# Causal mask added by VectorE instead of a TensorE product, row maximum subtracted by GpSimd, two engine orders rearranged, in one attention layer of a decoder kernel

## The chip, the cores and the metric

The kernel runs on one core of one Trainium2 chip. The core has TensorE (PE: matmuls, and PEld for its weight loads), VectorE (DVE), ScalarE (ACT), GpSimd (POOL) and the queue engine SyncE (SP), each with an instruction queue of its own that is worked off strictly in order. They meet only at semaphores. The metric is device time in microseconds (us) of one launch; lower is better.

## The reference, cut to what matters

Two decoder layers with a layer norm after every residual sum. The fourth and the fifth of the six blocks are attentions of 16 heads of 16 elements, over 16 sequences of 128 tokens and 256 channels. The fourth has no mask; the fifth reads keys and values from a context and is causal:

```python
q = x @ Wq.T;  k = context @ Wk.T;  v = context @ Wv.T        # split into 16 heads
scores = jnp.einsum('bhqd,bhkd->bhqk', q, k) * SCALE
causal = jnp.tril(jnp.ones((t, kv_t), dtype=bool))
scores = jnp.where(causal[None, None, :, :], scores, -jnp.inf)
probs = jax.nn.softmax(scores, axis=-1)
y = jnp.einsum('bhqk,bhkd->bhqd', probs, v)
return y.transpose(0, 2, 1, 3).reshape(b, t, c) @ Wo.T + bo
```

Then `x = layernorm(x + y)`. All of it is fp32.

## The kernel before, in words

Each block is a round of 16 turns, one sequence each. The two attentions are round D (`n == 0`, no mask) and round E (`n == 1`, causal). They are written by one piece of code and run as one unbroken pipeline: `chained` walks through iterations, and in iteration i each engine runs its list of stages in the order of that list, a stage of lag L on turn i - L. So the position in an engine's list is its queue order within an iteration, and the lags say which of the five sequences in flight a stage belongs to. Buffers named with `[t.p]` are double; PSUM banks are not: bank 1 takes the projections of q and k, bank 2 v and the output projection, banks 3 to 6 the scores of four heads each (r = 0 to 3), bank 7 the transposed probabilities, bank 0 the weighted values.

One turn goes through these stages, with lags in brackets:

- `turn_x` (0) transposes x, `copy_xT` (0) copies it out; `d_proj_` (1) computes q and k, `d_qkc_` (1, ScalarE) copies them out in four instructions, `d_kx_` (1, GpSimd) expands k.
- `d_scores_` (2): in round E four mask products first, line 1232 (identity times the causal table, both bf16, 512 columns each, one for each bank), then 16 products with 32 rows, line 1237, which add to the banks.
- `d_max_(r)` (2, VectorE), for r = 0 to 3: the maximum over a row from the bank (line 1986), then the bank minus the maximum into `d_S` in SBUF (line 1989).
- `d_exp_(r)` (r = 0, 1, 2 at lag 2, r = 3 at lag 3; ScalarE, line 1557): exponential in place.
- `d_pT_(r)` (3, TensorE, line 1251): four transposes into bank 7. `d_pTc_(r)` (3, ScalarE, line 1564) copies bank 7 out. There is one bank 7, so `d_pT_(r + 1)` waits for `d_pTc_(r)`.
- `d_pv_` (3, line 1261) multiplies with v into bank 0; `d_oTc_` (4, ScalarE, line 1571) copies it out; `d_back_` (4) transposes it back; `d_div_` (4, VectorE, lines 1997 and 1999) divides by the row sums; `d_atp_`, `d_atc_`, `d_out_` (4) make the output projection; `d_y_` (4, VectorE) adds the residual (line 2007) and then runs the statistics of the layer norm (lines 1664, 1673); `ln_power` (4, GpSimd, lines 781 and 783) takes the root; `ln_final` (4, VectorE, line 1681) normalises.

TensorE's list per iteration, which the change leaves as it is, is: transposes r = 0 (lag 3), projection (1), back (4), transposes r = 1 (3), scores (2), atp (4), transposes r = 2 (3), v (1), transposes r = 3 (3), output projection (4), turn of x (0), pv (3). ScalarE's list ends with `d_exp_(2)`, and the next iteration begins with `d_oTc_` and `d_pTc_(0)`. GpSimd's list is copy of x, `d_xb_` (residual plus bias), `d_kx_`, `ln_power`.

SyncE issues loads of inputs and weights for later rounds during round E; they hang on semaphores that the change does not touch, apart from one small table (`rid`) whose semaphore is merged into another.

Of the kernel before, what the change touches and what calls it, by code (L numbers as in the profile page):

```python
# [268 lines left out]
def build(nc, a):  # L269
    out = a["out"]  # L270
    with ExitStack() as ctx:
# [16 lines left out]
        ident_bf = sb("ident_bf", [P, P], BF16)  # L288
        causal_bf = sb("causal_bf", [P, P], BF16)
# [199 lines left out]
        l_rid = sem("l_rid")  # L489
# [110 lines left out]
        d_max = step("d_max", 2 * NQ)  # L600
        d_exp = step("d_exp", NQ)
# [57 lines left out]
        def _(sp):  # L659
# [40 lines left out]
            sp.dma_start(rid[:], a["rid"]).then_inc(l_rid, 16)  # L700
# [66 lines left out]
        def _(pool):  # L767
# [104 lines left out]
            pool.wait_ge(l_rid, 16)  # L872
# [43 lines left out]
        def _(pe):  # L916
# [276 lines left out]
            for n, round in enumerate((D_, E_)):  # L1193
# [31 lines left out]
                def d_scores_(t, n=n):  # L1225
                    wait(pe, d_kxc.again(n), t, KC)
                    wait(pe, d_qkc.again(n), t, 4)
                    for r in range(NQ):
                        o = bank[3 + r]
                        wait(pe, d_max.again(n), t, 2 * (r + 1), back=1)  # L1230
                        if n == 1:
                            pe.matmul(o[:].rearrange("p (a b) -> p a b", a=QH), ident_bf[:],  # L1232
                                      causal_bf[:].unsqueeze(1).to_broadcast([P, QH, P]), start=True, stop=False)
                    for k in range(KC):
                        for r in range(NQ):
                            part = slice(32 * r, 32 * r + 32)
                            m = pe.matmul(bank[3 + r][:, k * D:(k + 1) * D], d_qT[t.p][part, k, :],  # L1237
                                          d_kx[t.p][part, k].rearrange("p a b -> p (a b)"), start=n == 0,
                                          stop=n == 0 or k == KC - 1)
# [99 lines left out]
            for i in range(B + 2):  # L1339
# [6 lines left out]
                if i == ROUTED_AFTER:  # L1346
                    pe.wait_ge(f_pre, 1)
                    pe.wait_ge(l_fc, 16)
# [44 lines left out]
        def _(act):  # L1393
# [146 lines left out]
            for n, round in enumerate((D_, E_)):  # L1540
# [39 lines left out]
                rounds.append([(d_oTc_, 4), (d_pTc_(0), 3), (d_exp_(3), 3), (d_qkc_, 1), (d_pTc_(1), 3), (d_atc_, 4),  # L1580
# [70 lines left out]
        def _(dve):  # L1651
# [37 lines left out]
            dve.tensor_copy(ident_bf[:], ident)  # L1689
            dve.tensor_copy(causal_bf[:], c("causal"))  # L1690
# [277 lines left out]
            for n, round in enumerate((D_, E_)):  # L1968
# [11 lines left out]
                def d_max_(r, n=n):  # L1980
                    dm = d_max.again(n)
                    def stage(t):
# [3 lines left out]
                        dve.tensor_reduce(mx, s_, AX.X, ALU.max).then_inc(dm.sem, 1)  # L1986
                        wait(dve, dm, t, 2 * r + 1)
                        wait(dve, d_pTp.again(n), t, NQ, back=2)
                        dve.tensor_tensor(d_S[t.p][:, QH * r:QH * (r + 1), :], s_,  # L1989
                                          mx.unsqueeze(2).to_broadcast([P, QH, P]), ALU.subtract).then_inc(dm.sem, 1)  # L1990
# [20 lines left out]
                rounds.append([(d_div_, 4), (d_max_(0), 2), (d_max_(1), 2), (d_max_(2), 2), (d_y_, 4), (d_max_(3), 2),  # L2011
# [36 lines left out]
            dve.wait_ge(l_fc, 16)  # L2048
# [215 lines left out]
```

## Time and profile before

| what | us |
|---|---|
| median of 3 runs | 1096.15 (1089.13 to 1096.21) |
| the profiled execution, its own time | 1097.09 |
| its span from first to last instruction | 1095.3 |
| PE busy | 930.2 (85%) |
| DVE busy | 593.5 (54%) |
| ACT busy | 444.4 (41%) |
| POOL busy | 432.5 (39%) |

Times in rows are microseconds from the start of the span, durations within a group of equal instructions are nanoseconds. Ends of matmuls are modelled, so consecutive PE rows overlap a little; the distance of two starts is the time that the first one really took from the queue.

### The profile page before, as it was taken

To read this page: it belongs to the slowest core of one execution; us is meant where nothing else is said; L and a number is where in the kernel's file an instruction comes from. 1 tells how busy PE (TensorE), PEld (TensorE's weight loads), DVE (VectorE), ACT (ScalarE), POOL (GpSimd) and SP (SyncE) were. 2 spreads that over 40 slices of the span, in tenths; PEclk is the share of its full clock that TensorE was granted. 3 is DMA by queue.
4 is the path that set the end of the run, shared out by engine and by line. 5 is a ranking of instruction groups with operands and counts; after the bars stand their busy time and mean duration, and the time that the engine had idled before them with its cause. 6 is when DMAs were issued, how large, how long until landed. Compare 5 with 4: busy or idle time off the path is not lost.

```text
span 1095.3 us, 20796 instructions
## 1 busy us (share of the span) xinstructions
PE 930.2 (85%) x5702; PEld 655.9 (60%) x5703; DVE 593.5 (54%) x1516; ACT 444.4 (41%) x1145; POOL 432.5 (39%) x678
## 2 busy tenths in 40 slices
PE   5888797784876899999999979989429999999980
PEld 2655686562754788888778757546205555555550
DVE  2898576647135888887778754731102222222224
ACT  2444332332201777776666644223203332233323
POOL 4799233200024233332223310067744554455553
PEclk8999997687585999999999986999759999999995
DMA  6500017900001000001322104023333445544546
GB/s 239 205 20 24 10 40 230 263 3 1 1 0 61 2 1 0 0 6 45 102 93 84 58 27 176 20 88 114 113 99 62 83 86 88 88 80 88 85 65 239
DMA packets 69845, 84.54 MB, mean 77 GB/s; under 512 B 16288, under 2 KB 61216, under 8 KB 69280
## 3 DMA queue, kind: packets, MB, share of 16 engines
q1 hardware_dynamic: 54624, 62.24, 18.8%
q0 software_dynamic: 14448, 19.01, 9.8%
q10 hardware_dynamic: 720, 2.63, 0.6%
q8 instruction: 26, 0.43, 0.2%
q14 instruction: 27, 0.22, 0.1%
HBM read 47.95 MB, written 36.24 MB: 77 GB/s over the span
## 4 chain that ended last, share of the span: by engine, by line
PE 65%; POOL 12%; DVE 8%; issue 7%; DMA 3%; ACT 2%; POOLq 0%; DVEq 0%; SPq 0%; ACTq 0%
PE bank L933 40%; PE bank L946 6%; POOL grid L886 6%; PE bank L1251 6%; PE bank L1237 3%; PE bank L1261 3%; PE bank L1232 1%; PE bank L1144 1%; POOL arena L803 1%; DMA inT<-in_xT 1%; POOL lr L783 1%; PE bank L925 1%; POOL arena L798 1%; POOL arena L797 1%; PE bank L1301 1%
## 5 line engine op out<-in xcount | busy, mean ns | idle before, releaser
L933 PE MATMUL bank<-arena 128*128 (+6 forms) x1248 | 416.5, 475 | 24.2 <-ACT arena L1444 10.5
L933 PEld LDWEIGHTS bank<-arena 128*128 128x128 f32 (+1 forms) x1248 | 229.4, 203 | 131.4 <-issue 87.8
L896 POOL DMA_INDIRECT ys<-arena x79 | 123.0, 1557 | 136.6 <-DVE arena L2155 127.5
L946 PEld LDWEIGHTS bank<-const,arena 128*128 128x128 f32 x636 | 77.3, 141 | 106.8 <-issue 99.1
L946 PE MATMUL bank<-const,arena 128*128 128x128 f32 x636 | 103.5, 277 | 37.6 <-DMA arena<-grid 32.3
L2147 DVE SCALAR_TENSOR_TENSOR arena<-arena,bank 128x256 f32<-128x256 f32 x79 | 38.0, 481 | 178.8 <-ACT arena L1627 178.8
L1986 DVE TENSOR_REDUCE arena<-bank 128x4 f32<-128x512 f32 x128 | 87.5, 683 | 37.4 <-PE bank L1237 37.2
L781 POOL TENSOR_TENSOR lr<-mv,const 128x1 f32<-128x1 f32 x80 | 15.2, 190 | 234.3 <-DVE mv L1673 234.3
L1627 ACT ACTIVATE arena<-bank 128x256 f32<-128x256 f32 x79 | 30.3, 383 | 174.6 <-PE bank L933 174.6
L933 PE MATMUL bank<-arena,inT 128*128 128x256 f32 (+1 forms) x256 | 85.3, 460 | 17.3 <-DMA inT<-in_xT 8.4
L1557 ACT ACTIVATE arena<-arena 128x512 f32<-128x512 f32 x128 | 80.9, 632 | 44.4 <-DVE arena L1989 40.7
L1989 DVE TENSOR_TENSOR arena<-bank,arena 128x512 f32<-128x512 f32 x128 | 88.6, 692 | 6.5
L933 PE MATMUL bank<-xT,arena 128*128 128x128 f32 x576 | 84.2, 295 | 5.2 <-ACT arena L1486 2.4
L1251 PE MATMUL bank<-const,arena 128*128 128x128 f32 x512 | 80.2, 280 | 2.8 <-ACT arena L1564 1.9
L933 PEld LDWEIGHTS bank<-xT,arena 128*128 128x128 f32 x576 | 75.9, 207 | 11.3 <-issue 5.3
L1564 ACT COPY arena<-bank 128x512 f32<-128x512 f32 x128 | 75.5, 590 | 8.0 <-PE bank L1251 4.4
L886 POOL DMA_INDIRECT grid<-arena x64 | 63.1, 986 | 27.0 <-issue 14.6
L1251 PEld LDWEIGHTS bank<-const,arena 128*128 128x128 f32 x512 | 56.5, 142 | 19.5 <-issue 18.0
L933 PEld LDWEIGHTS bank<-arena,inT 128*128 128x128 f32 x256 | 45.8, 198 | 34.7 <-issue 17.0
L853 POOL TENSOR_TENSOR arena<-arena,const 128x256 f32<-128x256 f32 x64 | 37.9, 612 | 35.3 <-ACT arena L1547 35.3
L2155 DVE COPY arena<-bank 128x256 f32<-128x256 f32 x79 | 33.6, 425 | 33.5 <-PE bank L933 33.5
L1416 ACT COPY xT<-bank 128x256 f32<-128x256 f32 x64 | 23.5, 367 | 65.9 <-DVE arena L1966 37.3
(259 smaller groups left out, 1371.7 us busy)
## 6 DMA issues: line engine op xcount, KB each, us to landing
arena<-in_f_w SPq DMA_DIRECT2D x18, 768.0 KB, 4.5
arena<-grid SPq DMA_DIRECT2D x79, 132.0 KB, 2.1
grid<-arena SPq DMA_DIRECT2D x1, 10112.0 KB, 33.2
inT<-in_ctxT SPq DMA_DIRECT2D x32, 128.0 KB, 2.0
arena<-ys SPq DMA_DIRECT2D x8, 512.0 KB, 6.3
inT<-in_xT SPq DMA_DIRECT2D x16, 128.0 KB, 2.1
X<-in_x SPq DMA_DIRECT2D x1, 2048.0 KB, 8.4
arena<-in_c_w SPq DMA_DIRECT2D x2, 1024.0 KB, 5.4
```

Source lines behind the costliest of these rows:

```text
L853: pool.tensor_tensor(d_kx[t.p][:, k], d_kT[t.p][:, k:k + 1, :].to_broadcast([P, 2, P]), c("pairs").unsqueeze(2).to_broadcast([P, 2, P]), A ...
L886: pool.indirect_dma_start(grid, bass.IndirectOffsetOnAxis(ap=f_to[:, b, k:k + 1], axis=0), f_sg[i][:, k, :], None).then_inc(l_sc[i], 16)
L896: pool.indirect_dma_start(ys, bass.IndirectOffsetOnAxis(ap=number, axis=0), s_y[t.ring(YR)], None, compute_op=ALU.add).then_inc(l_sy[t.rin ...
L933: m = pe.matmul(o, lhs[k], rhs[k], start=k == 0, stop=k == n - 1)
L946: m = pe.transpose(o[:, k * width:(k + 1) * width], src(k), ident[0:width, 0:width])
L1251: m = pe.transpose(bank[7][:, i * P:(i + 1) * P], d_S[t.p][:, QH * r + i, :], ident)
L1557: act.activation(v, v, ACT.Exp).then_inc(d_exp.sem, 1)
L1564: act.copy(d_pT[t.p][:, QH * r:QH * (r + 1), :], bank[7][:].rearrange("p (a b) -> p a b", a=QH)).then_inc(d_pTc.sem, 1)
L1986: dve.tensor_reduce(mx, s_, AX.X, ALU.max).then_inc(dm.sem, 1)
L1989: dve.tensor_tensor(d_S[t.p][:, QH * r:QH * (r + 1), :], s_, mx.unsqueeze(2).to_broadcast([P, QH, P]), ALU.subtract).then_inc(dm.sem, 1)
L2147: dve.scalar_tensor_tensor(out=f_a[0][:, t.p * EF:(t.p + 1) * EF], in0=f_h[t.p], scalar=s_x[t.ring(SR)][:, D:D + 1], in1=bank[2 + t.p][:, ...
L2155: dve.tensor_copy(s_y[t.ring(YR)], bank[6 + t.p][:, 0:D]).then_inc(q_yc.sem, 1)
```

## The change

The mask products of round E go, and with them the two bf16 tables and the two casts that filled them. In round E VectorE adds the causal table to the scores while it copies them from the bank to `d_S`, then takes the maximum from `d_S`; the subtraction becomes a new stage `d_sub_(r)` on GpSimd, in place in `d_S` (128 x 512), and the exponential waits for it. Round D keeps its two VectorE instructions. Both rounds take over new orders: VectorE does `d_y_` before `d_max_(2)` rather than after it; ScalarE does `d_qkc_` before `d_exp_(3)`. GpSimd's list becomes `d_sub_(3)` at lag 3, copy of x, `d_xb_`, `d_kx_`, `d_sub_(0)`, `d_sub_(1)`, `ln_power`, `d_sub_(2)`. The wait for `rid` is merged into that for `f_const`.

```diff
                 def d_scores_(t, n=n):
...
                     for r in range(NQ):
-                        o = bank[3 + r]
                         wait(pe, d_max.again(n), t, 2 * (r + 1), back=1)
-                        if n == 1:
-                            pe.matmul(o[:].rearrange("p (a b) -> p a b", a=QH), ident_bf[:],
-                                      causal_bf[:].unsqueeze(1).to_broadcast([P, QH, P]), start=True, stop=False)
...
+                def d_sub_(r, n=n):
+                    def stage(t):
+                        if n == 1:
+                            wait(pool, d_max.again(1), t, 2 * r + 2)
+                            v = d_S[t.p][:, QH * r:QH * (r + 1), :]
+                            pool.tensor_tensor(v, v, d_mx[t.p][:, QH * r:QH * (r + 1)].unsqueeze(2)
+                                               .to_broadcast([P, QH, P]), ALU.subtract).then_inc(d_sub.sem, 1)
+                    return stage
...
-                rounds.append([(copy_x(round, round - 1), 0), (d_xb_, 3), (d_kx_, 1), (ln_power(round), 4)])
+                rounds.append([(d_sub_(3), 3), (copy_x(round, round - 1), 0), (d_xb_, 3), (d_kx_, 1), (d_sub_(0), 2),
+                               (d_sub_(1), 2), (ln_power(round), 4), (d_sub_(2), 2)])
...
                 def d_exp_(r, n=n):
                     def stage(t):
-                        wait(act, d_max.again(n), t, 2 * r + 2)
+                        if n == 0:
+                            wait(act, d_max.again(0), t, 2 * r + 2)
+                        else:
+                            wait(act, d_sub, t, r + 1)
...
-                rounds.append([(d_oTc_, 4), (d_pTc_(0), 3), (d_exp_(3), 3), (d_qkc_, 1), (d_pTc_(1), 3), (d_atc_, 4),
+                rounds.append([(d_oTc_, 4), (d_pTc_(0), 3), (d_qkc_, 1), (d_exp_(3), 3), (d_pTc_(1), 3), (d_atc_, 4),
...
+                        v = d_S[t.p][:, QH * r:QH * (r + 1), :]
+                        if n == 0:
...
+                        else:
+                            wait(dve, d_pTp.again(n), t, NQ, back=2)
+                            dve.tensor_tensor(v, s_, c("causal").unsqueeze(1).to_broadcast([P, QH, P]), ALU.add)\
+                               .then_inc(dm.sem, 1)
+                            wait(dve, dm, t, 2 * r + 1)
+                            wait(dve, d_sub, t, NQ, back=2)
+                            dve.tensor_reduce(mx, v, AX.X, ALU.max).then_inc(dm.sem, 1)
...
-                rounds.append([(d_div_, 4), (d_max_(0), 2), (d_max_(1), 2), (d_max_(2), 2), (d_y_, 4), (d_max_(3), 2),
+                rounds.append([(d_div_, 4), (d_max_(0), 2), (d_max_(1), 2), (d_y_, 4), (d_max_(2), 2), (d_max_(3), 2),
                                (d_vc_, 1), (ln_final(round), 4)])
```

VectorE in round E, before, from the first maximum of an iteration on (banks 3 to 6 are r = 0 to 3, `y0` is the residual sum and waits for the output projection, `d_op`):

```order
L1986 TENSOR_REDUCE arena<-bank3 128x4 [waits d_sp]
L1989 TENSOR_TENSOR arena<-bank3,arena 128x512 [waits d_pTp,d_max]
L1986 TENSOR_REDUCE arena<-bank4 128x4 [waits d_sp]
L1989 TENSOR_TENSOR arena<-bank4,arena 128x512 [waits d_pTp,d_max]
L1986 TENSOR_REDUCE arena<-bank5 128x4 [waits d_sp]
L1989 TENSOR_TENSOR arena<-bank5,arena 128x512 [waits d_pTp,d_max]
L2007 TENSOR_TENSOR y0<-bank2,arena 128x256 [waits normed,d_xbc,d_op]
L1664 BN_STATS bn0<-y0 128x6 [waits d_y]
L1673 BN_AGGR mv0<-bn0 128x2 [waits rstd,stats]
L1986 TENSOR_REDUCE arena<-bank6 128x4 [waits d_sp]
L1989 TENSOR_TENSOR arena<-bank6,arena 128x512 [waits d_pTp,d_max]
```

and of the change, the same place (lines are numbered as in the changed kernel):

```order
L2000 TENSOR_TENSOR arena<-bank3,const 128x512 [waits d_pTp,d_sp]
L2004 TENSOR_REDUCE arena<-arena 128x4 [waits d_sub,d_max]
L2000 TENSOR_TENSOR arena<-bank4,const 128x512 [waits d_pTp,d_sp]
L2004 TENSOR_REDUCE arena<-arena 128x4 [waits d_sub,d_max]
L2021 TENSOR_TENSOR y0<-bank2,arena 128x256 [waits normed,d_xbc,d_op]
L1671 BN_STATS bn0<-y0 128x6 [waits d_y]
L1680 BN_AGGR mv0<-bn0 128x2 [waits rstd,stats]
L2000 TENSOR_TENSOR arena<-bank5,const 128x512 [waits d_pTp,d_sp]
L2004 TENSOR_REDUCE arena<-arena 128x4 [waits d_sub,d_max]
L2000 TENSOR_TENSOR arena<-bank6,const 128x512 [waits d_pTp,d_sp]
L2004 TENSOR_REDUCE arena<-arena 128x4 [waits d_sub,d_max]
```

The residual sum with its statistics has moved ahead of the pair on bank 5, and the add now comes ahead of the maximum.

ScalarE in round E, before, from `d_exp_(2)` at the end of one iteration into the next:

```order
L1557 ACTIVATE arena<-arena 128x512 [waits d_max]
L1571 COPY arena<-bank0 128x512 [waits d_bk,d_pv]
L1564 COPY arena<-bank7 128x512 [waits d_pv,d_pTp]
L1557 ACTIVATE arena<-arena 128x512 [waits d_max]
L1547 ACTIVATE arena<-bank1 128x128 [waits d_sp,d_kxc,d_qkp]
L1547 ACTIVATE arena<-bank1 128x128
L1550 ACTIVATE arena<-bank1 128x128 x2
L1564 COPY arena<-bank7 128x512 [waits d_pv,d_pTp]
```

and of the change:

```order
L1564 ACTIVATE arena<-arena 128x512 [waits d_sub]
L1578 COPY arena<-bank0 128x512 [waits d_bk,d_pv]
L1571 COPY arena<-bank7 128x512 [waits d_pv,d_pTp]
L1551 ACTIVATE arena<-bank1 128x128 [waits d_sp,d_kxc,d_qkp]
L1551 ACTIVATE arena<-bank1 128x128
L1554 ACTIVATE arena<-bank1 128x128 x2
L1564 ACTIVATE arena<-arena 128x512 [waits d_sub]
L1571 COPY arena<-bank7 128x512 [waits d_pv,d_pTp]
```

The exponentials (now line 1564) wait for GpSimd; the one of r = 2 still stands last in the iteration, ahead of the two copies that open the next; the one of r = 3 has moved behind the four copies of q and k.

GpSimd in round E, of the change, one iteration (before, it held only lines 773, 861, 853, 781 and 783, which are 771, 868, 851, 779 and 781 here). The first row is `d_sub_(2)` of one iteration and `d_sub_(3)` of the next:

```order
L860 TENSOR_TENSOR arena<-arena 128x512 [waits d_max] x2
L771 COPY xs0<-X 128x256 [waits turned,normed]
L868 TENSOR_TENSOR arena<-X,rows 128x256 [waits normed,d_y]
L851 TENSOR_TENSOR arena<-arena,const 128x256 [waits d_qkc,d_sp]
L851 TENSOR_TENSOR arena<-arena,const 128x256
L860 TENSOR_TENSOR arena<-arena 128x512 [waits d_max] x2
L779 TENSOR_TENSOR lr0<-mv0,const 128x1 [waits normed,stats]
L781 TENSOR_TENSOR lr0<-lr0,const 128x1 [waits rstd]
```

Four subtractions of 512 columns have come in, the one of r = 2 behind `ln_power`.

## Rows read from the trace of the kernel before

**Rows 1.** Stretches of rounds D and E: length, busy PE, PEld, DVE, ACT, POOL; clock
```profile
356.00:490.00 134.00, 131.24 (x1447) 109.25 (x1446) 115.35 (x225) 104.17 (x230) 43.17 (x89) 1.00 0.01 2
492.00:634.00 142.00, 141.39 (x1487) 112.37 (x1485) 113.25 (x225) 95.81 (x224) 43.39 (x88) 1.00 0.23 74
```

**Rows 2.** Mask and score products: count, ns min/median/max, first and last start
```profile
L1232 PE MATMUL bank<-causal_bf,ident_bf x64: 378/379/380, 491.9 to 633.8; 128*128 128x512 bf16 x64
L1237 PE MATMUL bank<-arena x512: 373/374/479, 354.6 to 634.8; 32*128 32x256 f32 x171
```

**Rows 3.** Timeline of PE in round E: start, us, engine, line, tiles, count
```profile
559.27 1.15 PE L1237 MATMUL bank<-arena 32*128 32x256 f32 x16
...
562.45 1.03 PE L933 MATMUL bank<-arena 128*128 128x256 f32 x4
...
567.36 0.60 PE L1251 MATMUL bank<-const,arena 128*128 128x128 f32 x4
567.80 1.03 PE L1232 MATMUL bank<-causal_bf,ident_bf 128*128 128x512 bf16 x4
568.75 1.15 PE L1237 MATMUL bank<-arena 32*128 32x256 f32 x16
```

**Rows 4.** Timeline of DVE in round E, the same turn; brackets: idle before, releaser
```profile
560.43 0.69 DVE L1986 TENSOR_REDUCE arena<-bank 128x4 f32<-128x512 f32 x1 [1.39 <-PE bank L1237]
...
563.19 0.68 DVE L1986 TENSOR_REDUCE arena<-bank 128x4 f32<-128x512 f32 x1
563.91 0.69 DVE L1989 TENSOR_TENSOR arena<-bank,arena 128x512 f32<-128x512 f32 x1
564.52 0.41 DVE L2007 TENSOR_TENSOR y<-bank,arena 128x256 f32<-128x256 f32 x1
...
565.65 0.69 DVE L1986 TENSOR_REDUCE arena<-bank 128x4 f32<-128x512 f32 x1
```

**Rows 5.** Timeline of ACT in round E, exponential of r = 2 and what follows
```profile
564.63 0.63 ACT L1557 ACTIVATE arena<-arena 128x512 f32<-128x512 f32 x1 [0.43 <-DVE arena L1989]
...
565.64 0.59 ACT L1564 COPY arena<-bank 128x512 f32<-128x512 f32 x1
...
567.64 0.43 ACT L1547 ACTIVATE arena<-bank 128x128 f32<-128x128 f32 x2
...
568.26 0.61 ACT L1564 COPY arena<-bank 128x512 f32<-128x512 f32 x1
```

**Rows 6.** Timeline of PE in round D, from one group of scores to the next
```profile
422.56 1.15 PE L1237 MATMUL bank<-arena 32*128 32x256 f32 x16
...
423.92 0.60 PE L1251 MATMUL bank<-const,arena 128*128 128x128 f32 x4
...
425.75 1.03 PE L933 MATMUL bank<-arena 128*128 128x256 f32 x4
...
430.65 0.60 PE L1251 MATMUL bank<-const,arena 128*128 128x128 f32 x4
431.19 1.15 PE L1237 MATMUL bank<-arena 32*128 32x256 f32 x16
```

**Rows 7.** Timeline of ACT in round D, the same turn
```profile
427.93 0.63 ACT L1557 ACTIVATE arena<-arena 128x512 f32<-128x512 f32 x1 [0.43 <-DVE arena L1989]
...
430.93 0.61 ACT L1547 ACTIVATE arena<-bank,cols 128x128 f32<-128x128 f32 x2
...
431.93 0.60 ACT L1564 COPY arena<-bank 128x512 f32<-128x512 f32 x1
```

**Rows 8.** GpSimd: elementwise on 512 and on 256 columns: ns min/median/max, first and last
```profile
L803 POOL TENSOR_TENSOR arena<-arena x16: 1255/1451/1715, 14.3 to 105.6; 128x512 f32<-128x512 f32 x16
L853 POOL TENSOR_TENSOR arena<-arena,const x64: 611/612/615, 351.2 to 625.7; 128x256 f32<-128x256 f32 x64
```

**Rows 9.** Timeline, round D: normalisation on DVE beside GpSimd's add
```profile
430.61 0.59 DVE L1681 TENSOR_SCALAR X<-y,mv,lr 128x256 f32 x1
430.31 0.74 POOL L861 TENSOR_TENSOR arena<-X,rows 128x256 f32<-128x256 f32 x1
```

More of the change, by code:

```diff
@@ L287, in build @@
         cols = sb("cols", [P, N_COLS])
-        ident_bf = sb("ident_bf", [P, P], BF16)
-        causal_bf = sb("causal_bf", [P, P], BF16)
         xs = [sb(f"xs{i}", [P, D]) for i in range(2)]
@@ L488, in build @@
         l_inT = [sem("l_inT0"), sem("l_inT1")]
-        l_rid = sem("l_rid")
         l_fill = sem("l_fill")
@@ L600, in build @@
         d_max = step("d_max", 2 * NQ)
+        d_sub = step("d_sub", NQ)
         d_exp = step("d_exp", NQ)
@@ L699, in _ @@
             load_x(turn(7))
-            sp.dma_start(rid[:], a["rid"]).then_inc(l_rid, 16)
+            sp.dma_start(rid[:], a["rid"]).then_inc(l_fc, 16)
             sp.dma_start(c_mask, a["mask"]).then_inc(l_cw, 16)
@@ L871, in _ @@
             pool.wait_ge(f_tail.sem, 3)
-            pool.wait_ge(l_rid, 16)
+            pool.wait_ge(l_fc, 32)
             pool.wait_ge(l_fill, 16 * 4)
@@ L1237, in d_scores_ @@
                             m = pe.matmul(bank[3 + r][:, k * D:(k + 1) * D], d_qT[t.p][part, k, :],
-                                          d_kx[t.p][part, k].rearrange("p a b -> p (a b)"), start=n == 0,
-                                          stop=n == 0 or k == KC - 1)
+                                          d_kx[t.p][part, k].rearrange("p a b -> p (a b)"), start=True,
+                                          stop=True)
                             if k == KC - 1:
@@ L1347, in _ @@
                     pe.wait_ge(f_pre, 1)
-                    pe.wait_ge(l_fc, 16)
+                    pe.wait_ge(l_fc, 32)
                     flat = lambda v: v.rearrange("p b e -> p (b e)")
@@ L1688, in _ @@
             dve.wait_ge(l_const, 16)
-            dve.tensor_copy(ident_bf[:], ident)
-            dve.tensor_copy(causal_bf[:], c("causal"))
             dve.memset(f_fill, 0.0).then_inc(f_filled, 1)
@@ L1985, in stage @@
                         mx = d_mx[t.p][:, QH * r:QH * (r + 1)]
[L1986 to L1990, printed above, removed]
+                        v = d_S[t.p][:, QH * r:QH * (r + 1), :]
+                        if n == 0:
+                            dve.tensor_reduce(mx, s_, AX.X, ALU.max).then_inc(dm.sem, 1)
+                            wait(dve, dm, t, 2 * r + 1)
+                            wait(dve, d_pTp.again(n), t, NQ, back=2)
+                            dve.tensor_tensor(v, s_, mx.unsqueeze(2).to_broadcast([P, QH, P]), ALU.subtract)\
+                               .then_inc(dm.sem, 1)
+                        else:
+                            wait(dve, d_pTp.again(n), t, NQ, back=2)
+                            dve.tensor_tensor(v, s_, c("causal").unsqueeze(1).to_broadcast([P, QH, P]), ALU.add)\
+                               .then_inc(dm.sem, 1)
+                            wait(dve, dm, t, 2 * r + 1)
+                            wait(dve, d_sub, t, NQ, back=2)
+                            dve.tensor_reduce(mx, v, AX.X, ALU.max).then_inc(dm.sem, 1)
                     return stage
@@ L2047, in _ @@
             grp = lambda v: v.rearrange("p b (g e) -> p (b g) e", e=EPG)
-            dve.wait_ge(l_fc, 16)
+            dve.wait_ge(l_fc, 32)
             route(dve.tensor_tensor(f_s, f_sc, row("ebias").unsqueeze(1).to_broadcast([P, B, E]), ALU.add))
```

## Prediction, written before the changed kernel was run

> **What bounds the kernel now.** I read the stretches first. In both rounds TensorE is never idle (131.2 of 134 us, 141.4 of 142), VectorE is busy 86% and 80%, ScalarE 78% and 67%, GpSimd about 3 us a turn, at clock 1.00 [rows 1]. The starts of the products give the periods: round D from 354.6 to 491.9, 16 iterations, 8.58 us each; round E from 491.9 to 633.8, 15 iterations, 9.46 us each [rows 2]. The timeline of one turn says the same: scores to scores 9.48 us in E, 8.63 in D [rows 3, 6], and the four mask products hold TensorE for 567.80 to 568.75, 0.95 us [rows 3], which is the difference. So TensorE sets the end now, and it is the engine that is relieved.
>
> A busy share says nothing of how far the next limit is, so I then followed the ring that closes through the other engines. Take s, the start of the score products, as zero.
>
> Round E before: VectorE starts on bank 3 at 1.16 and on bank 5 at 3.92; that pair ends at 564.60, 5.33 [rows 4]. The exponential of r = 2 starts at 564.63, 5.36. Behind it in ScalarE's queue stand the copy of bank 0 and then the copy of bank 7, which starts 1.01 behind the exponential (565.64) and is over 1.60 behind it, at 566.23 or 6.96 [rows 5]. TensorE's transposes of r = 1 need that copy; they start at 567.36, 8.09 [rows 3]. The ring has 1.13 us of slack, and it returns to the scores 0.44 us behind 567.36, plus the mask's 0.95. In D the same exponential starts at 5.37 and the transposes at 430.65, again 8.09 [rows 6, 7].
>
> **The change part by part.**
>
> *Mask products gone.* -0.95 us an iteration on TensorE. If nothing else bound, E would run at 9.48 - 0.95 = 8.53.
>
> *VectorE's pairs.* Bank minus maximum (0.69) becomes bank plus table, maximum from the bank (0.68) becomes maximum from SBUF. No row shows that maximum here; bounds are 0.61, the distance from 563.91 to 564.52 at which a 512-column operation lets the next one start, and 0.69. I take 0.68, nothing gained. A pair stays 1.41 long (563.19 to 564.60) [rows 4].
>
> *The residual sum ahead of bank 5, in both rounds.* It waits for the output projection of its iteration, whose modelled end is 562.45 + 1.03 = 563.48, 4.21 behind s in E, and 426.78, 4.22, in D [rows 3, 6]. With 0.05 us to cross, it starts at 4.26. VectorE is there at 3.92 [rows 4], so it now idles 0.34 us, and then spends 564.52 to 565.65 = 1.13 us on sum and statistics. The pair on bank 5 starts at 4.26 + 1.13 = 5.39 instead of 3.92. Everything queued behind it on ScalarE (the exponential of r = 2, both copies) is later by 1.47, and the next transposes on TensorE wait for those copies.
>
> *The subtraction on GpSimd, E alone.* No row shows it. Nearest are 256 columns with broadcast operands at 0.612, so 1.22 for two, and 512 plain columns of two operands at 1.255 at best, 1.451 in the median, 1.715 at worst [rows 8]. I take 1.25, the undisturbed one, and 0.1 for the extra crossing; the range keeps 1.2 and 1.72. The Trainium skill (GPSIMD Engine Reference, Performance versus the Vector engine) has a two-input fp32 operation on GpSimd take 1.96 times VectorE's time; an estimate by it is 1.36 us, which would add 0.11 us an iteration to the sum. No run here shows that ratio.
> GpSimd's load becomes 3.0 + 4 x 1.25 = 8.0 us an iteration: under every period below, so its latency counts and not its throughput. In queue order, the one of r = 2 finds `ln_power` done before it.
>
> *Round E, summed.* Bank 5's pair ends at 5.39 + 1.41 = 6.80; subtraction to 8.15; exponential at 8.20 instead of 5.36; bank 7 copied at 8.20 + 1.60 = 9.80; transposes at 9.85 instead of 8.09; scores 0.44 later at 10.29. Against 9.48 this is +0.81 us: the stall of 1.76 eats the 0.95 and more.
>
> *Round D, summed.* By the same ring without GpSimd the exponential starts at 6.84 instead of 5.37, transposes at 8.49, +0.40. A longer ring runs through the other reordering. Behind the copy of bank 7 now stand the four copies of q and k, 430.93 to 431.93 = 1.00 us [rows 7], and then the exponential of r = 3, which used to fit into ScalarE's idle time. From the exponential of r = 2: +1.01 copy of bank 7, +1.51 q and k, +2.51 exponential, +3.05 second copy of bank 7, +3.65 done, +3.70 transposes of r = 2, then 423.92 to 426.78 = 2.86 us to the end of the output projection [rows 6], 0.05 to the residual sum, and 1.13 + 1.41 + 0.04 back to the exponential: 9.19 us. D goes from 8.63 to 9.19, +0.56. In E this ring takes 10.17 (the copies of q and k take only 567.64 to 568.26 = 0.62 there [rows 5]), so the first one binds.
>
> *The rest.* Two casts of 128 columns at the start and a merged semaphore: at most the 0.69 us of one 512-column operation [rows 4]; I count nothing, since it ends up in the rounding. Loads by SyncE in E have no wait that the change moves. Removing `d_exp_(3)` from in front of the copies of q and k helps `d_kx_`, which has an iteration of slack. At the end of E the last sequence runs without cover: +1.35 for its subtraction, +0.3 idle before it, -0.95 for its mask: +0.7.
>
> Sum: D has residual sums from its third interval on, 14 x 0.56 = 7.8; E 15 x 0.81 = 12.2; end 0.7; together +20.7 on the profiled execution's own 1097.09, 1117.8. That execution lies 0.94 over the median of the runs, so 1116.9; I say **1116.5 us**, slower by 1.9%.
>
> **The rivals.**
>
> *TensorE stays the bound (faster).* If the ring's additions were covered, E would run at 8.53: 15 x 0.95 = 14, and 1082 us. TensorE's unbroken busy time in rows 1 speaks for it. Against it: the ring must not grow by more than 1.13 - 0.95 = 0.18 us in E, and the subtraction alone is 1.25. Chance 0.10.
>
> *The additions half hold (no change).* If the residual sum did not wait (the output projection done by 3.92) and statistics overlapped, only GpSimd's 1.35 would count: E at 9.48 - 0.95 + 1.35 - 0.18 = 9.70, D 8.9, and 1096 + 3 + 4 = 1103. I find no row in favour; modelled ends of matmuls, which could be off by 0.2 us, are the only opening. Chance 0.11.
>
> *VectorE and GpSimd block each other (slower still).* In D the normalisation ran beside GpSimd's add of 430.31 to 431.05 and ended at 431.20, 0.15 behind it; its 0.59 us look like a wait for the neighbour [rows 9]. Now the maxima read SBUF while subtractions run. If they exclude each other, the maximum of r = 1, due at 3.3, waits until the subtraction of r = 0 ends near 3.95; the residual sum starts at 4.75 instead of 4.26, E takes 10.8, and the time is 1117 + 15 x 0.5 = 1124. The same result comes if the subtraction takes its 1.72: 15 x 0.47 = 7. For it: the 0.59, and the spread in rows 8. Against: a maximum has a single SBUF operand. Chance 0.17.
> The Trainium skill (SBUF — State Buffer, section SBUF: two separate sides) says that the two engines share one pair of ports, held for a whole instruction by a GpSimd operation or by a VectorE one that uses two SBUF inputs or a two-port mode. By that rule the normalisation waits and the maximum does not; the normalisation has cover here, since the division behind it waits for ScalarE's copy of bank 0 until 9.98, so the rule would leave the forecast where it is. Rows 9 agree with it for the normalisation.
>
> *The clock falls* because TensorE now idles 1 to 2 us an iteration. Both rounds were granted 1.00 without a gap [rows 1], so these rows cannot price it; it would act in the same direction as the third rival and shares its chance.
>
> **How the numbers follow.** Forecast 0.62, the others 0.10, 0.11, 0.17. Its own spread: subtraction 1.2 and maximum 0.60 give 15 x -0.13 = -2; half of D's effect -4; matmul ends 0.2 earlier in both rounds -6. So 1105 to 1120. The range takes in the blocked case with some room above and most of the no-change case below, and leaves out the faster one: 1101 to 1126. A measurement of this kernel tells 1% from no change. Faster 0.10; same 0.12 (the half-held case and a thin edge of the forecast); slower 0.78.
>
> **What would show it.** Right: scores to scores 10.3 us in E and 9.2 in D; ScalarE idle before the exponential of r = 2, released by GpSimd in E; TensorE idle before the transposes of r = 1 (line 1251) by 1.5 to 1.8 us in E and before those of r = 1 or 2 in D, released by ScalarE's bank 7 copy; VectorE idle about 0.3 us before the residual sum, released by TensorE. Wrong: if TensorE has no idle time in E and its period is near 8.5, the ring is not there; if D is still at 8.6, the reordering costs nothing and all of the loss or gain is E's; if the subtraction takes 1.5 us or more, or a maximum stretches beside it, the third rival holds.

## The result, and the profile after

The changed kernel takes 1123.8 us in the median of 4 runs (1119.18 to 1127.36) against 1095.8 us: 1.0268 times the time of before, 95% interval 1.0212 to 1.0323. The forecast was 1116.5 us, slower by 1.9%, in a range of 1101 to 1126. The profiled execution took 1127.36 us, 30.3 more than that of before; it is the longest of the four.

The stretches of rounds D and E in the changed kernel (columns as in [rows 1]):

```profile
356.00:499.00 143.00, 136.13 (x1445) 109.18 (x1444) 114.75 (x224) 100.97 (x227) 43.51 (x90) 1.00 0.01 2
499.00:661.00 162.00, 140.26 (x1462) 112.37 (x1460) 128.26 (x235) 96.01 (x230) 106.33 (x150) 0.98 0.19 65
```

and its score products (as in [rows 2]; the line of the mask products has no counterpart):

```profile
L1241 PE MATMUL bank<-arena x512: 374/374/792, 354.0 to 658.9; 32*128 32x256 f32 x171
```

TensorE, unbroken before, is now idle 6.9 us in D and 21.7 us in E. To see where the time lies, I take the starts of the 32 groups of score products (one group for each turn, so the distance of two is an iteration) from each kernel's timeline of TensorE, and the first transpose of the stage behind the attentions (line 1301 before, 1305 after). D is from the first group to the 17th (16 intervals), E from the 17th to the 32nd (15), the end from the 32nd to that transpose.

| us | D | E | end | steady iteration in D / E |
|---|---|---|---|---|
| before | 138.3 | 141.2 | 20.2 | 8.6 to 8.8 / 9.48 |
| changed | 147.4 | 156.1 | 26.5 | 9.3 to 9.5 / 10.4 |
| forecast for the change | +7.8 | +12.2 | +0.7 | 9.19 / 10.29 |
| measured | +9.1 | +14.9 | +6.3 | |

Together +30.2; D started 0.6 earlier than before, and the later stages add the same again.

One turn of round E follows, from the timelines of the changed kernel; rows between are left out where three dots stand. TensorE (before: [rows 3]):

```profile
563.18 1.15 PE L1241 MATMUL bank<-arena 32*128 32x256 f32 x16
...
566.36 1.03 PE L941 MATMUL bank<-arena 128*128 128x256 f32 x4
...
568.37 1.08 PE L1265 MATMUL bank<-arena 128*32 128x128 f32 x32 [0.76 <-ACT arena L1571]
...
572.46 0.66 PE L954 MATMUL bank<-const,arena 128*128 128x128 f32 x4 [0.64 <-ACT arena L1578]
573.04 0.63 PE L1255 MATMUL bank<-const,arena 128*128 128x128 f32 x4
573.63 1.15 PE L1241 MATMUL bank<-arena 32*128 32x256 f32 x16
```

VectorE (before: [rows 4]):

```profile
564.44 0.69 DVE L2000 TENSOR_TENSOR arena<-bank,const 128x512 f32<-128x512 f32 x1 [0.94 <-PE bank L1241]
...
566.60 0.69 DVE L2004 TENSOR_REDUCE arena<-arena 128x4 f32<-128x512 f32 x1
567.52 0.42 DVE L2021 TENSOR_TENSOR y<-bank,arena 128x256 f32<-128x256 f32 x1 [0.23 <-PE bank L941]
...
568.74 0.69 DVE L2000 TENSOR_TENSOR arena<-bank,const 128x512 f32<-128x512 f32 x1
569.46 0.69 DVE L2004 TENSOR_REDUCE arena<-arena 128x4 f32<-128x512 f32 x1
...
571.71 1.02 DVE L1688 TENSOR_SCALAR X<-y,mv,lr 128x256 f32 x1
```

GpSimd, the subtractions of r = 0, r = 2 and r = 3:

```profile
566.05 1.04 POOL L860 TENSOR_TENSOR arena<-arena 128x512 f32<-128x512 f32 x1 [1.77 <-DVE arena L2004]
...
570.23 1.04 POOL L860 TENSOR_TENSOR arena<-arena 128x512 f32<-128x512 f32 x1 [0.51 <-DVE arena L2004]
571.55 1.04 POOL L860 TENSOR_TENSOR arena<-arena 128x512 f32<-128x512 f32 x1 [0.28 <-DVE arena L2004]
```

ScalarE (before: [rows 5]):

```profile
571.30 0.63 ACT L1564 ACTIVATE arena<-arena 128x512 f32<-128x512 f32 x1 [1.97 <-POOL arena L860]
571.84 0.57 ACT L1578 COPY arena<-bank 128x512 f32<-128x512 f32 x1
572.30 0.59 ACT L1571 COPY arena<-bank 128x512 f32<-128x512 f32 x1
```

The ring (the chain of waits from TensorE's scores through the other engines' queues and back to TensorE) can be walked in these rows. A bracket gives the time from the scores at 563.18, and then the forecast. The residual sum waits for the output projection and starts at 567.52 (+4.34; 4.26). The pair on bank 5 starts 1.22 later and ends at 570.15 (+6.97; 6.80). GpSimd subtracts from 570.23 to 571.27 (+8.09; 8.15), the exponential of r = 2 starts at 571.30 (+8.12; 8.20; before 5.36). Bank 0's copy stands behind it, and TensorE, idle 0.64 us, takes up the transposes back when that is over, then those of r = 1 at 573.04 (+9.86; 9.85), then the scores at 573.63 (+10.45; 10.29). TensorE's wait stands one step ahead of where I had put it: before line 954, whose data is bank 0's copy, not before line 1255. Its size is also another. I had forecast 1.5 to 1.8 us in one place; there are two waits, this one of 0.64 us and one of 0.76 us before the product with v (line 1265), which waits for bank 7's last copy. The second belongs to another ring, which experiments 4 and 5 uncover.

Round D, changed kernel, TensorE's timeline and then ScalarE's (before: [rows 6, 7]):

```profile
425.51 0.65 PE L954 MATMUL bank<-const,arena 128*128 128x128 f32 x4 [0.31 <-ACT arena L1578]
426.09 0.63 PE L1255 MATMUL bank<-const,arena 128*128 128x128 f32 x4
426.73 1.15 PE L1241 MATMUL bank<-arena 32*128 32x256 f32 x16
```

```profile
424.35 0.63 ACT L1564 ACTIVATE arena<-arena 128x512 f32<-128x512 f32 x1 [2.13 <-DVE arena L1996]
```

Score products start at 417.26 and again at 426.73, 9.47 us later; the exponential of r = 2 waits 2.13 us for VectorE and starts 7.09 behind the scores, where it was 5.37 [rows 6, 7].

### The profile page after: what moved, and what is told of

It is laid out like the page before. It is cut to its first block, busy times and chain, and to the rows that moved or that the text cites. A ratio compares the mean times of both kernels' runs of the same rounds, so it can differ in the third digit from the quotient of the medians.

```text
span 1125.5 us, 20843 instructions
## 1 busy us (share of the span) xinstructions
PE 932.1 (83%) x5638; PEld 654.4 (58%) x5639; DVE 603.2 (54%) x1514; ACT 441.4 (39%) x1145; POOL 498.7 (44%) x742
## 4 chain that ended last, share of the span: by engine, by line
PE 51%; POOL 14%; DVE 12%; issue 11%; ACT 4%; DMA 1%; POOLq 1%; DVEq 0%; ACTq 0%; SPq 0%
PE bank L941 32%; PE bank L954 6%; POOL grid L894 6%; PE bank L1255 4%; PE bank L1241 3%; POOL arena L860 2%; POOL lr L781 2%; DVE bn L1671 2%; ACT arena L1578 1%; PE bank L1152 1%; DVE arena L1996 1%; DVE arena L1993 1%; DVE y L2021 1%; POOL arena L801 1%; PE bank L1305 1%
## 5 line engine op out<-in xcount | busy, mean ns | idle before, releaser
L954 PE MATMUL bank<-const,arena 128*128 128x128 f32 x636 | 106.8, 282 | 53.7 <-DMA arena<-grid 33.0
L1634 ACT ACTIVATE arena<-bank 128x256 f32<-128x256 f32 x79 | 30.3, 383 | 174.6 <-PE bank L941 166.0
L860 POOL TENSOR_TENSOR arena<-arena 128x512 f32<-128x512 f32 x64 | 66.7, 1043 | 47.1 <-DVE arena L2004 47.1
L1255 PE MATMUL bank<-const,arena 128*128 128x128 f32 x512 | 83.5, 287 | 3.3 <-ACT arena L1571 2.3
L941 PEld LDWEIGHTS bank<-xT,arena 128*128 128x128 f32 x576 | 76.7, 208 | 11.3 <-issue 5.3
L1571 ACT COPY arena<-bank 128x512 f32<-128x512 f32 x128 | 75.8, 592 | 11.3 <-PE bank L1255 9.0
L1993 DVE TENSOR_REDUCE arena<-bank 128x4 f32<-128x512 f32 x64 | 43.7, 682 | 17.9 <-PE bank L1241 17.5
L2000 DVE TENSOR_TENSOR arena<-bank,const 128x512 f32<-128x512 f32 x64 | 43.9, 686 | 16.4 <-PE bank L1241 16.4
L1688 DVE TENSOR_SCALAR X<-y,mv,lr 128x256 f32 (+1 forms) x80 | 42.9, 537 | 16.0 <-POOL lr L781 14.8
```

The source lines that it names most:

```text
L860: pool.tensor_tensor(v, v, d_mx[t.p][:, QH * r:QH * (r + 1)].unsqueeze(2) .to_broadcast([P, QH, P]), ALU.subtract).then_inc(d_sub.sem, 1)
L941: m = pe.matmul(o, lhs[k], rhs[k], start=k == 0, stop=k == n - 1)
L954: m = pe.transpose(o[:, k * width:(k + 1) * width], src(k), ident[0:width, 0:width])
L1255: m = pe.transpose(bank[7][:, i * P:(i + 1) * P], d_S[t.p][:, QH * r + i, :], ident)
L1571: act.copy(d_pT[t.p][:, QH * r:QH * (r + 1), :], bank[7][:].rearrange("p (a b) -> p a b", a=QH)).then_inc(d_pTc.sem, 1)
L1688: dve.tensor_scalar(o, y[t.p][:], mv[t.p][:, 0:1], lr[t.p][:, 1:2], ALU.subtract, ALU.mult)\
```

## Experiments

**1. VectorE's order alone, on the kernel before.**

```diff
-                rounds.append([(d_div_, 4), (d_max_(0), 2), (d_max_(1), 2), (d_max_(2), 2), (d_y_, 4), (d_max_(3), 2),
+                rounds.append([(d_div_, 4), (d_max_(0), 2), (d_max_(1), 2), (d_y_, 4), (d_max_(2), 2), (d_max_(3), 2),
```

> The kernel before, with one edit: VectorE does the residual sum and its statistics ahead of the pair on bank 5 (r = 2) in both rounds. Theory (the ring through ScalarE's queue): the exponential of r = 2 starts 7.1 us behind the scores instead of 5.4, the transposes of r = 1 about 1.74 behind it, scores again 0.6 later in D and 1.55 later in E, where the mask products stand between: D at 9.4 to 9.5 us an iteration, E at 10.2 to 10.4, 1118 to 1124 us in all. So this order alone would cost as much as the whole change. Rival (the order is harmless and the loss is GpSimd's): 1094 to 1099 us, periods of 8.6 and 9.5.

Measured: 1115.9 us, 1.0205 (1.0156 to 1.0254). D 147.8, E 151.5, iterations of 9.3 to 9.5 and of 10.0 to 10.1. The last interval of E, 11.2, is not among them. Its timelines of ScalarE and TensorE in E show the same ring without GpSimd:

```profile
574.57 0.63 ACT L1557 ACTIVATE arena<-arena 128x512 f32<-128x512 f32 x1 [1.91 <-DVE arena L1989]
575.11 0.57 ACT L1571 COPY arena<-bank 128x512 f32<-128x512 f32 x1
```

```profile
575.73 0.66 PE L946 MATMUL bank<-const,arena 128*128 128x128 f32 x4 [0.18 <-ACT arena L1571]
```

So one stage moved in a list costs 2%, and the rival, that the order is harmless, is out. In D it costs the whole of what the change costs there (147.8 against 147.4). The total came out 2 us under the expected range, since E's iteration was 10.05 where I had put 10.2 to 10.4.

**2. ScalarE's order alone, on the kernel before.**

```diff
-                rounds.append([(d_oTc_, 4), (d_pTc_(0), 3), (d_exp_(3), 3), (d_qkc_, 1), (d_pTc_(1), 3), (d_atc_, 4),
+                rounds.append([(d_oTc_, 4), (d_pTc_(0), 3), (d_qkc_, 1), (d_exp_(3), 3), (d_pTc_(1), 3), (d_atc_, 4),
```

> The kernel before, with one edit: ScalarE copies q and k (1.0 us in D, 0.62 in E) ahead of the exponential of r = 3, in both rounds. Theory: both stand ahead of bank 7's second copy in either order, so nothing changes: 1093 to 1098 us, D 8.6, E 9.5. Rival (the second step of the prediction for D, that this reordering lengthens a ring): D at 9.0 to 9.2 us and 1102 to 1106 us.

Measured: 1098.2 us, 1.0035 (1.0015 to 1.0054); D 141.8 with iterations of 8.96, E unchanged at 9.48. Neither theory was right as written: the first had no effect at all, the rival had 1102 to 1106 us. The reordering costs D 0.2 to 0.3 us an iteration, by a ring that neither had. ScalarE's timeline in D, then TensorE's one turn earlier:

```profile
428.36 0.62 ACT L1547 ACTIVATE arena<-bank,cols 128x128 f32<-128x128 f32 x2 [1.36 <-PE bank L933]
428.88 0.63 ACT L1550 ACTIVATE arena<-bank,arena 128x128 f32<-128x128 f32 x2
429.38 0.65 ACT L1557 ACTIVATE arena<-arena 128x512 f32<-128x512 f32 x1
429.89 0.60 ACT L1564 COPY arena<-bank 128x512 f32<-128x512 f32 x1
```

```profile
421.67 0.63 PE L1251 MATMUL bank<-const,arena 128*128 128x128 f32 x4 [0.15 <-ACT arena L1564]
```

ScalarE waits 1.36 us for the projection, then does the copies of q and k (1.0), the exponential of r = 3 and bank 7's copy, for which TensorE waits. In the kernel before, ScalarE did the exponential of r = 3 first:

```profile
430.40 0.63 ACT L1557 ACTIVATE arena<-arena 128x512 f32<-128x512 f32 x1 [0.88 <-DVE arena L1989]
```

It waited there for VectorE and began while the projection was just ending (modelled end 430.38, and in this experiment the copies start 0.19 behind that end), so about a third of it was hidden. The ring was nearly closed already: every second iteration of D took 8.78 before. In E the copies take 0.62 and the slack covers it.

**3. The changed kernel with VectorE's order of before.**

```diff
-                rounds.append([(d_div_, 4), (d_max_(0), 2), (d_max_(1), 2), (d_y_, 4), (d_max_(2), 2), (d_max_(3), 2),
+                rounds.append([(d_div_, 4), (d_max_(0), 2), (d_max_(1), 2), (d_max_(2), 2), (d_y_, 4), (d_max_(3), 2),
```

> The changed kernel with VectorE's order of before (residual sum behind the pair on bank 5). Theory: D returns to 8.6 us an iteration (13 us back). E does not: on GpSimd the layer norm's root stands ahead of the subtraction of r = 2 and now waits for statistics that come at 6.45 us behind the scores, so the subtraction runs from 7.3 to 8.4, and E takes 10.6 to 10.9 instead of 10.4. Together 1112 to 1118 us. Rival (VectorE's order is the whole loss): E at 8.9 and 1088 to 1096 us.

Measured: 1122.0 us, 1.0247 (1.0208 to 1.0286), 4 us over the expected range. E 161.8, iterations of 10.6 to 10.9 as expected; D 141.0 at 8.97, not 8.6, which is experiment 2's effect. The rival, that VectorE's order is the whole loss, is out: taking that order back wins 6 us in D and loses as much in E. GpSimd's timeline shows the queue (the last row holds the subtractions of r = 2 and r = 3), and VectorE's the normalisation:

```profile
575.87 0.19 POOL L779 TENSOR_TENSOR lr<-mv,const 128x1 f32<-128x1 f32 x1 [1.40 <-DVE mv L1680]
576.14 0.55 POOL L781 TENSOR_TENSOR lr<-lr,const 128x1 f32<-128x1 f32 x1
576.66 2.10 POOL L860 TENSOR_TENSOR arena<-arena 128x512 f32<-128x512 f32 x2
```

```profile
577.45 0.41 DVE L1688 TENSOR_SCALAR X<-y,mv,lr 128x256 f32 x1
```

Two small operations of a layer norm wait 1.40 us for statistics, and the subtraction of r = 2, ready at 574.67 where its maximum ended, starts at 576.66. With GpSimd's order as the change has it, the residual sum has to stand early on VectorE: the two orders belong together.

**4. As 3, and GpSimd subtracts r = 2 ahead of the layer norm.**

```diff
-                               (d_sub_(1), 2), (ln_power(round), 4), (d_sub_(2), 2)])
+                               (d_sub_(1), 2), (d_sub_(2), 2), (ln_power(round), 4)])
```

> As a_dve, and on GpSimd the subtraction of r = 2 ahead of the layer norm's root. Theory: the exponential of r = 2 starts at 6.5 us behind the scores, E takes 8.8 to 9.0 us an iteration, D 8.6, and the time is 1086 to 1093 us, faster than before. Rival (GpSimd's load and its collisions with VectorE bind E whatever the order): E stays over 9.5 us and the time over 1096.

Measured: 1095.0 us, 1.0001 (0.9978 to 1.0025), 2 us over the expected range. The loss is gone by two positions in two lists; the one on GpSimd's list alone is worth 27 us against experiment 3. D is at 8.96 again, and E comes to 9.46 where I expected 8.9. The next ring, in the timelines of ScalarE and TensorE:

```profile
566.09 0.63 ACT L1564 ACTIVATE arena<-arena 128x512 f32<-128x512 f32 x1 [1.37 <-POOL arena L860]
566.63 0.57 ACT L1571 COPY arena<-bank 128x512 f32<-128x512 f32 x1
```

```profile
567.34 1.08 PE L1265 MATMUL bank<-arena 128*32 128x128 f32 x32 [0.76 <-ACT arena L1571]
```

The exponential of r = 0 stands in front of bank 7's last copy; GpSimd's subtraction holds it 1.37 us, with it the copy behind it, and so the product with v on TensorE for 0.76 us. It is the same kind of ring, one place on, and its two waits stood in the changed kernel already, inside the longer iteration.

**5. The changed kernel, the exponential of r = 2 behind the two copies.** This is the one test with the subtraction in place in which VectorE's and GpSimd's orders stay as the change has them.

```diff
-                rounds.append([(d_oTc_, 4), (d_pTc_(0), 3), (d_qkc_, 1), (d_exp_(3), 3), (d_pTc_(1), 3), (d_atc_, 4),
+                rounds.append([(d_oTc_, 4), (d_pTc_(0), 3), (d_exp_(2), 3), (d_qkc_, 1), (d_exp_(3), 3), (d_pTc_(1), 3), (d_atc_, 4),
                                (d_pTc_(2), 3), (d_exp_(0), 2), (d_pTc_(3), 3), (d_exp_(1), 2),
-                               (copy_xT(round, before, reader, bank[1]), 0), (d_exp_(2), 2)])
+                               (copy_xT(round, before, reader, bank[1]), 0)])
```

> The changed kernel with one edit: on ScalarE the exponential of r = 2 runs at lag 3, behind the two copies (bank 0, bank 7) that TensorE's next products wait for. Theory (that exponential, late by VectorE's order and GpSimd's subtraction, holds the copies up): TensorE's waits before the transposes back (line 954) go. E then falls to the next ring, about 9.45 us an iteration (exponential of r = 0 in front of bank 7's last copy, TensorE waits 0.76 us before line 1265), D to 8.9 to 9.0 us. 1098 to 1104 us. Rival (the subtraction's time or its collisions bind as such, wherever the exponential stands): E stays at 10.2 to 10.5 and the time over 1115.

Measured: 1097.7 us, 1.0013 (0.9973 to 1.0054); D 141.1 at 8.96, E 139.8 at 9.45, and TensorE's only wait in E is the 0.76 us of experiment 4. A single stage of one engine, put behind two others, takes back the whole loss: the late exponential did its harm by standing ahead of two copies, not by being late.

**6. Without the subtraction.**

```diff
-                        if n == 1:
+                        if n == 2:
                             wait(pool, d_max.again(1), t, 2 * r + 2)
...
-                            wait(act, d_sub, t, r + 1)
+                            wait(act, d_max.again(n), t, 2 * r + 2)
...
+                        act.activation(v, v, ACT.Exp, scale=1.0 if n == 0 else 0.01).then_inc(d_exp.sem, 1)
...
-                            wait(dve, d_sub, t, NQ, back=2)
```

> The changed kernel without GpSimd's subtraction; the exponential waits for the maximum instead. It leaves out the subtraction of the maximum in round E and scales the exponential's argument by 0.01 there so that nothing overflows; all other instructions stand. Theory: the subtraction costs its own latency, 1.04 + 0.1 us, once an iteration on the ring: E 9.3 to 9.4 us, D unchanged at 9.4 to 9.5; 1103 to 1109 us. Also the normalisation on VectorE (1.02 us now) falls back to 0.4 to 0.6. Rival (VectorE's order alone sets E): E stays over 10 us, over 1115 in all.

Measured: 1105.4 us, 1.0106 (1.006 to 1.0153); E 138.7 at 9.25 to 9.33, D 147.4. So with these orders the subtraction on GpSimd costs 10.4 - 9.3 = 1.1 us an iteration, its 1.04 and one crossing (the time from one engine's end to the next one's start). The rest of E's loss, against the 8.62 that TensorE comes to in experiment 8, is order. The normalisation is back at 0.41, as expected.

**7. and 8. A ScalarE order for the new latency, and the normalisation moved.** The first has experiment 4's orders on VectorE and GpSimd, and this list in place of ScalarE's (the three lines that it replaces are left out):

```diff
+                rounds.append([(d_oTc_, 4), (d_pTc_(0), 3), (d_exp_(2), 3), (d_qkc_, 1), (d_pTc_(1), 3), (d_exp_(3), 3),
+                               (d_atc_, 4), (d_pTc_(2), 3), (d_pTc_(3), 3), (d_exp_(0), 2),
+                               (copy_xT(round, before, reader, bank[1]), 0), (d_exp_(1), 2)])
```

> a_dvepool with a ScalarE order for the subtraction's latency: bank 0's copy, bank 7's copy, exponential r = 2 (lag 3), q and k, bank 7's second copy, exponential r = 3, atp's copy, two copies of bank 7, exponentials r = 0 and r = 1. Theory: no exponential stands ahead of a copy for which TensorE waits before it is ready; D at 8.6 us, E limited by VectorE at 8.7 to 8.9 us (its instructions sum to 8.5 with the normalisation stretched to 1.0 beside GpSimd). 1082 to 1089 us, faster than before. Rival (there is another ring near 9.4 us): 1092 to 1097.

Measured: 1081.1 us, 0.9893 (0.985 to 0.9936), 1 us under the expected range. D 135.5 at 8.62; E 129.9, alternating 8.63 and 8.83. In E VectorE is now almost without a pause (3 us in the 110 from 510 us on), and one of its instructions runs beside a subtraction on GpSimd (timelines of the two):

```profile
563.43 1.02 DVE L1688 TENSOR_SCALAR X<-y,mv,lr 128x256 f32 x1
```

```profile
563.26 1.04 POOL L860 TENSOR_TENSOR arena<-arena 128x512 f32<-128x512 f32 x1 [0.51 <-DVE arena L2004]
```

The second moves that instruction one iteration on, to where VectorE waits for scores:

```diff
-                rounds.append([(d_div_, 4), (d_max_(0), 2), (d_max_(1), 2), (d_max_(2), 2), (d_y_, 4), (d_max_(3), 2),
-                               (d_vc_, 1), (ln_final(round), 4)])
+                rounds.append([(d_div_, 4), (ln_final(round), 5), (d_max_(0), 2), (d_max_(1), 2), (d_max_(2), 2), (d_y_, 4), (d_max_(3), 2),
+                               (d_vc_, 1)])
```

> best1 with the normalisation (line 1688) one iteration later, behind the division, where VectorE waits for scores anyway. Theory: if VectorE's stretched normalisation limits E in best1, E comes to 8.5 to 8.7 us, TensorE's own pace, 1080 to 1086 us. Rival: it does not limit, same as best1 within 2 us.

Measured: 1076.8 us, 0.9857 (0.9814 to 0.99), 3 us under the expected range; both rounds at 8.62 in every steady iteration, 135.5 and 128.5. In E the normalisation takes 0.41 and 0.57 in turn (VectorE's timeline, a short one):

```profile
562.52 0.41 DVE L1688 TENSOR_SCALAR X<-y,mv,lr 128x256 f32 x1
```

TensorE's timeline in the same iteration, the four transposes of r = 1 with the score products straight behind them:

```profile
561.68 0.60 PE L1255 MATMUL bank<-const,arena 128*128 128x128 f32 x4
562.21 1.15 PE L1241 MATMUL bank<-arena 32*128 32x256 f32 x16
```

**9. The same again, and a control.**

> best2 once more for a narrower interval: 1074 to 1080 us, 0.98 to 0.99 of the kernel before; D and E at 8.6 us an iteration.

Measured: 1077.4 us, 0.9831 (0.9798 to 0.9865).

The control has ScalarE's order and the place of the normalisation of experiment 8 on the kernel before, with the mask on TensorE and the subtraction on VectorE.

> The kernel before, mask products on TensorE and subtraction on VectorE, with the ScalarE order and the place of the normalisation of best2. Theory (TensorE limits E with the mask in it): E at 9.5 us, D at 8.6, 1091 to 1096 us; the gain of best2 then comes from the mask's removal and the orders only let it through. Rival (the orders alone bring it): 1078 to 1086 us.

Measured: 1090.8 us, 0.9952 (0.9926 to 0.9978). E stays at 9.48, D is at 8.62. So of the 18 us that experiment 8's kernel gains in this comparison, 5 are the orders and 13 come with the mask's removal: 15 x (9.48 - 8.62) = 12.9.

**10. The changed kernel again, for the end.**

> The changed kernel once more, unchanged. Question: where the last sequences of round E run without cover, TensorE took 26.5 us from its last scores to the first transposes of the next stage instead of 20.2, at a granted clock of 0.5 to 0.8. Theory A (the drop belongs to this kernel: its last full iterations idle 2.5 us, and the records fall to 0.50 right behind): again 24 to 27 us at a clock below 0.8, median 1119 to 1126 us. Theory B (which execution drops is chance): 19 to 21 us at a clock near 1.0, and a time near 1120 us.

Measured: 1122.9 us, 1.0251 (1.0214 to 1.0288). D 147.4 as in the first profile, E 155.3, 0.7 less and all of it in the last interval (10.24 against 11.01); the end took 22.3 us, between the two theories, so neither is right as written. Stretches of four microseconds of the first profile, then of this one (the third number from the right is the granted clock):

```profile
652.00:656.00 4.00, 1.54 (x26) 1.11 (x16) 3.71 (x6) 1.73 (x5) 3.12 (x5) 0.87 0.00 0
656.00:660.00 4.00, 4.00 (x26) 2.87 (x25) 1.17 (x3) 1.05 (x2) 0.37 (x1) 0.50 0.00 0
```

```profile
660.00:664.00 4.00, 1.67 (x36) 1.26 (x36) 3.73 (x8) 1.51 (x3) 2.60 (x5) 1.00 0.00 0
664.00:668.00 4.00, 2.62 (x14) 1.64 (x14) 0.68 (x2) 2.94 (x7) 1.46 (x2) 0.84 0.00 0
```

In the first the clock falls from full to half behind one wait of 2.46 us, at 655.5, in the second behind the second such wait, at about 666.5. The end is dearer than before in both, by 2.1 and 6.3 us, where I had said 0.7. The 4.2 us between the two executions go with the moment at which the clock falls. The kernel before loses clock there as well (0.66 to 0.81 from 642 us on), so its 20.2 holds some of it, and there the longest wait of TensorE up to the fall was 1.05 us.

## Why the prediction was right

**The direction and the place: right.** TensorE stopped being the bound, and the ring through ScalarE's in-order queue took over. Its stations were forecast within 0.17 us in E, in part by luck: errors of both signs cancel, as the next paragraphs show. The time alone would not have told. 1123.8 us lies above the forecast's own spread of 1105 to 1120, and on the 1124 of the third rival, whose mechanism the rows refute for the maxima.

**"The residual sum ahead of bank 5", +1.47 us on everything behind it: right, and 1.64.** The pair on bank 5 starts 5.56 behind the scores in E, where it was 3.92: the sum starts 0.08 later than forecast, and it takes 1.22 with its statistics where I had 1.13. Experiment 1 has this order alone: 1.0205, some 20 us. All of D's loss is its; in E, experiments 1 and 6 give 0.6 us an iteration to the order alone and 1.1 to the subtraction. Experiment 5 shows that both act through the queue.

**"The subtraction on GpSimd", 1.25 us: 1.04.** All 64 lie between 1.039 and 1.141, cheaper than both neighbours in [rows 8]; that is 1.5 times the 0.69 of VectorE's add, where the ratio of 1.96 that the prediction cites gives its 1.36. From the pair's end to the exponential it was 1.15 us instead of 1.40, an error of 0.25 in favour of the change.

**A missing term, the restart of TensorE.** Behind its wait the four transposes back take 0.58 us from start to start (572.46 to 573.04), where they take 0.44 in a full queue (566.92 to 567.36 before). With them the way from the exponential to the transposes of r = 1 is 1.74 instead of 1.65. The timelines of TensorE's weight loads show where it goes. Before, in the full queue, and then in the changed kernel, behind the wait:

```profile
566.81 0.47 PEld L946 LDWEIGHTS bank<-const,arena 128*128 128x128 f32 x4
```

```profile
572.46 0.42 PEld L954 LDWEIGHTS bank<-const,arena 128*128 128x128 f32 x4 [0.82 <-ACT arena L1578]
```

The loads ran 0.11 us ahead of the products (566.81 to 566.92); behind the wait both start at 572.46, since the loads wait for the same copy. That this lost lead is the whole 0.14 us is argued. The next four take 0.59, where I used 0.44, but most of that is not the restart: with the mask products gone the score products stand straight behind them, and there they take 0.53 in a full queue too (experiment 8; in D before it was 0.54, 430.65 to 431.19 [rows 6]). The sum is +0.17 - 0.25 + 0.09 + 0.15 = +0.16, 10.45 instead of 10.29. Over the first 14 intervals of E this makes 12.3 us instead of 11.3. The rest of E's miss is its last interval, 11.01 where it was 8.42 before: +2.6 instead of +0.8. In experiment 10, with the clock still full, it was 10.24, so 0.8 of that goes with the clock and 1.0 with the ring.

**"Mask products gone", -0.95: 0.86.** Where TensorE is the bound again, the iteration is 8.62 and not 8.53 (experiment 8), since the transposes ahead of the scores take 0.09 more there. The prediction's own periods had it, 9.48 - 8.63 = 0.85. It does not enter the result, in which the ring and not TensorE's work sets the period.

**Round D, "a longer ring runs through the other reordering", 9.19: wrong ring, size too small.** Experiment 1 gives 147.8 without that reordering, the change 147.4 with it; it adds nothing there. What holds D is the first ring, which I had at +0.40 and which measured +0.7 to +0.8: 7.09 instead of 6.84 for the exponential, then 1.74 instead of 1.65 to the transposes of r = 1, and 0.64 instead of 0.54 from there to the scores. That +7.8 came as near to the +9.1 as it did is luck. The reordering does cost 0.2 to 0.3 us when it is alone (experiment 2), by the wait for the projection, which I had not listed.

**The end, +0.7: 2.1 and 6.3 in two executions.** The term that missed by most. I had the latency and not the clock, and had given the clock no price of its own because [rows 1] show none.

**The rivals.** TensorE as the bound needed a ring that grows by less than 0.18 us; the exponential alone came 2.76 us later (5.36 to 8.12). The half-held case is out by experiment 1. Of the blocking of VectorE and GpSimd half is true. The normalisation does stretch, from the 0.41 of experiment 6 to 1.02, ending 0.14 behind the subtraction (571.71 to 572.73 beside 571.55 to 572.59). The maxima do not: all 64 take 0.685 to 0.689, that of 566.60 with a subtraction beside it from 566.05 to 567.09. So the rule cited from the Trainium skill (SBUF — State Buffer, section SBUF: two separate sides) held for both, as to which of the two waits, and in the changed kernel the stretch was covered, as argued: VectorE waits 0.41 us behind it, and the division starts at +9.97 (9.98). How long the wait is hangs on the moment. In experiment 3 the normalisation started 0.79 us into a subtraction that takes 1.04 and took only 0.41. By the rule it would have waited for the whole instruction, of whose recorded time 0.25 us were left; GpSimd's recorded times are rough, so this stays open. These two engines meet at more than semaphores, other than the section on the chip says. The stretch is no longer covered once the orders are mended, and costs E up to 0.2 us in every second iteration there (experiments 7 and 8).

## What to carry to other kernels

Taking 0.86 us an iteration off the busiest engine gained nothing as long as, in another engine's queue, an instruction that waited for a slow result stood in front of a ready one. Before such a change, follow the ring from the bound engine through each in-order queue and back, and compare its slack (here 1.13 us) with the latency added and with what is taken off; and when a latency grows, look for each instruction that waits for it and ask what is queued behind it that the bound engine needs sooner. A stage that is 100% busy tells only that its next limit is hidden: the removal paid 13 us, and the positions of a few stages in three lists decided whether it did.

## What the runs showed of the hardware that I had not expected

A GpSimd subtraction over 128 x 512 fp32, in place, with a per-group operand repeated 128 times, takes 1.04 us; the maximum from SBUF takes 0.69, as from a bank. A VectorE normalisation from SBUF to SBUF takes 1.02 us instead of 0.41 when it starts 0.16 us behind such a subtraction, and 0.41 when it starts 0.79 us behind it (experiment 3); the subtraction beside the long one keeps its 1.04. Four 128 x 128 fp32 transposes take 0.44 us from start to start in a full queue, and 0.58 behind a wait of 0.2 to 1.1 us. TensorE's clock held 1.00 through iterations with waits of 0.6 and 0.8 us in 10.4. It fell to half (1.2 GHz) behind waits of 2.5 us, not at the same one in two executions, and in the kernel before it fell at the end of E, at about 644 us, behind waits of at most 1.05 us.
